# A DLRM tower: tile 0 and the last tile in another order, and matmuls on a constant while TensorE waits for the first rows

## The reference

```python
e = jnp.stack([tbl_0[ids[:, 0]], ..., tbl_26[ids[:, 26]]], axis=1)     # 512 x 27 x 128
interactions = jnp.einsum('bfd,bgd->bfg', e, e)
z = jnp.concatenate([e.reshape(B, -1), interactions[:, _TRIU_I, _TRIU_J]], axis=1)
h = jnp.concatenate([z, dense_ctx], axis=1)                             # 512 x 3823
h = jnp.maximum(h @ W_top1 + b_top1, 0.0)                               # 512 x 512
h = jnp.maximum(h @ W_top2 + b_top2, 0.0)                               # 512 x 256
y = h @ W_top3
```

## Time and profile before

| | us |
|---|---|
| median of 3 runs (lowest, highest) | 192.55 (192.2, 193.46) |
| profiled execution, its own time | 192.25 |
| its span, first to last instruction | 190.5 |
| PE busy | 153.6 (81%) |
| DVE, ACT, POOL busy | 107.6, 106.3, 108.3 |
| mean granted TensorE clock | 0.973 |

### The profile page before, as it was taken

The page is one execution under the profiler, slowest core; times in us unless marked ns, Lnnn a source line. Parts: engine busy times, 40 slices in busy tenths (PEclk is TensorE's granted clock), DMA queues, the critical chain, the costliest instruction groups (busy, mean ns, idle before and its releaser), DMA issues.

```text
span 190.5 us, 2285 instructions
## 1 busy us (share of the span) xinstructions
PE 153.6 (81%) x744; PEld 135.4 (71%) x744; DVE 107.6 (57%) x204; ACT 106.3 (56%) x205; POOL 108.3 (57%) x114
## 2 busy tenths in 40 slices
PE   0033497709998798998999999999999999990885
PEld 0011376608997798897988989988989897970654
DVE  6664777726557975823684852358677203576201
ACT  2673768807459957434789341449836303498111
POOL 4878878787777778777577777766774000000000
PEclk9999999997999999999999999999999999999589
DMA  4988878862335422212122212221221000000000
GB/s 122 293 253 256 220 215 268 238 136 84 91 97 157 115 70 68 55 42 55 41 55 59 54 42 55 57 55 29 59 55 45 0 0 0 0 0 0 3 0 0
DMA packets 10021, 16.40 MB, mean 86 GB/s; under 512 B 3876, under 2 KB 4392, under 8 KB 9956
## 3 DMA queue, kind: packets, MB, share of 16 engines
q1 hardware_dynamic: 6553, 9.17, 15.8%
q0 software_dynamic: 3456, 7.08, 15.2%
HBM read 16.24 MB, written 0.00 MB: 85 GB/s over the span
## 4 chain that ended last, share of the span: by engine, by line
PE 55%; POOL 14%; ACT 10%; issue 8%; DMA 7%; DVE 4%; ACTq 0%
POOL rows L256 14%; PE h_ps L546 10%; PE h_ps L547 9%; PE h_ps L548 9%; ACT stage_a L306 6%; DMA rows<-in_tbl,ids_sb 6%; PE gram_ps L573 5%; PE gram_ps L612 4%; PE h_ps L586 4%; PE h_ps L588 4%; PE h_ps L587 4%; PE tp_ps L531 4%; ACT y L296 3%; DVE y L423 1%; DMA ids_sb<-in_ids 1%
## 5 line engine op out<-in xcount | busy, mean ns | idle before, releaser
L256 POOL DMA_INDIRECT rows<-in_tbl,ids_sb x108 | 107.6, 997 | 36.6 <-issue 30.8
L546 PE MATMUL h_ps<-w_hi,e 128*128 128x512 f32 x108 | 51.2, 475 | 0.0
L412 DVE TENSOR_TENSOR e<-tp_ps,e 128x512 fp32r<-128x512 f32 (+1 forms) x28 | 31.9, 1160 | 26.4 <-ACT e L280 14.4
L547 PE MATMUL h_ps<-w_lo,e 128*128 128x512 f32 x108 | 44.5, 412 | 0.0
L548 PE MATMUL h_ps<-w_hi,e 128*128 128x512 f32 x108 | 44.3, 410 | 0.0
L531 PE MATMUL tp_ps<-ident,rows 128*128 128x128 f32 x108 | 21.7, 304 | 27.1 <-DMA rows<-in_tbl,ids_sb 25.1
L280 ACT ACTIVATE e<-tp_ps 128x512 fp32r<-128x512 f32 (+1 forms) x28 | 28.7, 1056 | 23.0 <-PE tp_ps L531 18.5
L531 PEld LDWEIGHTS tp_ps<-ident,rows 128*128 128x128 f32 x108 | 14.4, 148 | 33.6 <-DMA rows<-in_tbl,ids_sb 19.6
L547 PEld LDWEIGHTS h_ps<-w_lo,e 128*128 128x128 f32 x108 | 33.7, 312 | 0.5
L548 PEld LDWEIGHTS h_ps<-w_hi,e 128*128 128x128 f32 x108 | 33.1, 306 | 0.6
L546 PEld LDWEIGHTS h_ps<-w_hi,e 128*128 128x128 f32 x108 | 33.0, 306 | 0.6
(11 more groups left out here) (43 smaller groups left out, 111.4 us busy)
## 6 DMA issues: line engine op xcount, KB each, us to landing
stage_a<-in_W_top SPq DMA_DIRECT2D x10, 512.0 KB, 4.2
rows<-in_tbl,ids_sb POOLq DMA_INDIRECT x108, 3.4
y<-in_W_top SPq DMA_DIRECT2D x3, 512.0 KB, 4.2
w<-in_W_top SPq DMA_DIRECT2D x1, 512.0 KB, 4.5
w_pairs<-in_W_top SPq DMA_DIRECT2D x11, 28.0 KB
w_pairs<-in_W_top SPq DMA_DIRECT2D x11, 24.0 KB
y<-in_W_top SPq DMA_DIRECT2D x1, 256.0 KB, 4.3
w_pairs<-in_W_top SPq DMA_DIRECT2D x5, 12.0 KB
```

The lines of the kernel that those rows point to most:

```text
L256: nc.gpsimd.indirect_dma_start(rows[:, n % RING, :], None, tables[f], bass.IndirectOffsetOnAxis(ids_sb[:, t, f:f + 1], 0), engine_sem=gath ...
L412: last = nc.vector.tensor_tensor(features(1, fs[0], fs[-1] + 1), tp_ps[k % 2][:, 0:len(fs), :], features(0, fs[0], fs[-1] + 1), ALU.subtract)
L546: nc.tensor.matmul(out, hi, w_hi[:, f, :], start=f == 0, stop=False)
L547: nc.tensor.matmul(out, hi, w_lo[:, f, :], start=False, stop=False)
```

## The change

- Tile 0: PE goes by single features: transpose of f, then the three matmuls of f - 6. Features 21 and 22 come ahead of gram, and four features are left for between its parts.
- Ahead of the first transpose PE does 14 matmuls of 512 columns on a constant, and two after each of the first six transposes; their output is read by no one. DVE sets the constant first (a memset of 640 elements a partition ahead of the one of `w_pairs`).
- The `spacer` memset writes 500 elements a partition, not 250.
- SP issues four pair loads behind each W_top1 load from feature 6 on, 44 of the 73, and the other 29 at the end.
- Last tile: quad 6 is transposed right after feature 12, the gram begins after feature 13 and `layer2(2)`, features 14 to 19 lie between its parts, and features 20 to 26 come after its last part, ahead of `pairs_h1(3)`. ACT and DVE do `split_e(3, 6)` earlier in their order. The outputs of `layer2(2)` and `layer3(2)` lie in other banks, and `copy_y(2)` comes after the second sum of tile 3.

```diff
-        h2T_ps = [gram_ps[:, 512 * m:512 * m + P] for m in range(MC)]
-        y_ps = gram_ps[0:1, 512 * MC:512 * MC + P]
+        def h2T_ps(t, m):
+            bank = m + 2 * (t == NT - 2)
+            return gram_ps[:, 512 * bank:512 * bank + P]
+        def y_ps(t):
+            return h1_ps[t % 2][0:1, 0:P] if t == NT - 2 else gram_ps[0:1, 512 * MC:512 * MC + P]
...
+        PAIRS_PER_W = 4
...
+            pair_loads = list(pair_weight_loads())
             for c in range(0, F, PER_DMA):
...
+                if c == 6:
+                    sp.wait_ge(pairs_zeroed, 1)
+                if c >= 6:
+                    for dst, src in pair_loads[PAIRS_PER_W * (c - 6) // PER_DMA:PAIRS_PER_W * (c - 4) // PER_DMA]:
+                        sp.dma_start(dst, src).then_inc(pairs_loaded, 16)
-            sp.wait_ge(pairs_zeroed, 1)
-            for dst, src in pair_weight_loads():
+            for dst, src in pair_loads[PAIRS_PER_W * (-(-F // PER_DMA) - 3):]:
                 sp.dma_start(dst, src).then_inc(pairs_loaded, 16)
...
                 else:
+                    split_e(t, 6)
                     copy_h1T(u)
                     relu_h2(u)
-                    split_e(t, 6)
...
-                nc.vector.memset(e[:, 0, 0:50, F:ROWS].bitcast(f32), 0.0).then_inc(spaced, 1)
+                nc.vector.memset(e[:, 0, 0:100, F:ROWS].bitcast(f32), 0.0).then_inc(spaced, 1)
...
+            nc.vector.memset(x[:, 0, 0:HC + 1, :].bitcast(f32), 1.0).then_inc(warm_ready, 1)
             nc.vector.memset(w_pairs[:, :, :], 0.0).then_inc(pairs_zeroed, 1)
...
                     copy_h1T(u)
+                    split_e(t, 6)
                     relu_h2(u)
-                    split_e(t, 6)
-                    copy_y(u)
             u = NT - 1
-            sums(u, 0, 5)
+            sums(u, 0, 2)
+            copy_y(u - 1)
+            sums(u, 2, 5)
...
+            def warm_up(n):
+                for _ in range(n):
+                    nc.tensor.matmul(h1_ps[1][:, :], x[:, 0, HC, :], x[:, 0, 0:HC, :].rearrange("p c b -> p (c b)"),
+                                     start=True, stop=True)
+            pe.wait_ge(warm_ready, 1)
+            warm_up(14)
+            for f in range(F):
+                transpose(0, f)
+                if f < 6:
+                    warm_up(2)
+                if f >= 6:
+                    embeddings_h1(0, f - 6, f - 5)
...
+                if u == 0:
+                    embeddings_h1(u, 21, 23)
+                    gram(u, 0)
+                    gram(u, 1)
+                    gram(u, 2)
+                    embeddings_h1(u, 23, 24)
+                    gram(u, 3)
+                    embeddings_h1(u, 24, 25)
+                    gram(u, 4)
+                    transposes(t, 0)
+                    gram(u, 5)
+                    embeddings_h1(u, 25, 26)
+                    gram(u, 6)
+                    embeddings_h1(u, 26, 27)
+                    gram(u, 7)
...
             u = NT - 1
-            grams(u)
+            transposes(u, 6)
+            transpose_h1(u - 1)
+            embeddings_h1(u, 13, 14)
+            layer2(u - 1)
+            gram(u, 0)
+            gram(u, 1)
+            layer3(u - 1)
+            embeddings_h1(u, 14, 15)
+            gram(u, 2)
...
+            embeddings_h1(u, 19, 20)
+            gram(u, 7)
+            embeddings_h1(u, 20, 27)
             pairs_h1(u)
```

More of the change, by code:

```diff
@@ L335, in relu_h2 @@
                 act.wait_ge(h2_done, MC * t + 1)
-                nc.scalar.activation(h2T[:, 0, :], h2T_ps[0], ACT.Relu, bias=b2[:, 0:1]).then_inc(h2_act_ready, 1)
+                nc.scalar.activation(h2T[:, 0, :], h2T_ps(t, 0), ACT.Relu, bias=b2[:, 0:1]).then_inc(h2_act_ready, 1)
             def sums(t, first, end):
@@ L521, in _, with transpose @@
         def _(pe):
-            def transposes(t, q):
+            def transpose(t, f):
+                q, i = divmod(f, QF)
                 k = t * NQ + q
-                if k == 0:
+                n = t * F + f
+                if n == 0:
                     pe.wait_ge(ident_ready, 1)
-                if k >= 2:
+                if k >= 2 and i == 0:
                     pe.wait_ge(e_lo_ready, k - 1)
[L528 to L532, removed]
+                pe.wait_ge(rows_landed[n % RING], 16 * (n // RING + 1))
+                last = nc.tensor.transpose(tp_ps[k % 2][:, i, :], rows[:, n % RING, :], ident[:, :])
+                if f == F - 1:
                     if t == 0:
@@ L535, in transposes, with embeddings_h1 @@
                     last = nc.tensor.transpose(tp_ps[k % 2][0:CTX, QF - 1, :], ctx_sb[:, t, :], ident[:, :])
[L536 to L542, removed]
+                if i == QF - 1 or f == F - 1:
+                    last.then_inc(transposed, 1)
+            def transposes(t, q):
+                for f in quad_features(q):
+                    transpose(t, f)
+            def embeddings_h1(t, first, end):
+                for f in range(first, end):
+                    if f == 0 and t >= 2:
+                        pe.wait_ge(h1_ready, 2 * (t - 1))
+                    if f % QF == 0:
+                        pe.wait_ge(e_lo_ready, t * NQ + f // QF + 1)
                     if t == 0:
@@ L560, in gram @@
                         pe.wait_ge(h1T_act_ready, t)
[L561 to L566, removed]
+                if part == 0 and t >= 2:
+                    pe.wait_ge(h2_act_ready, t - 1)
+                    pe.wait_ge(h2_dve_ready, t - 1)
+                if part == 1 and t >= 2:
+                    pe.wait_ge(y_ready, t - 1)
+                if part == 1 and t == NT - 1:
+                    pe.wait_ge(h2_act_ready, t)
+                    pe.wait_ge(h2_dve_ready, t)
                 if part >= 2:
@@ L611, in layer2 @@
                             pe.wait_ge(y_sum_ready, GP * (t + 2) - 1)
-                        last = nc.tensor.matmul(h2T_ps[m], w2[:, c, m * P:(m + 1) * P], h1T[:, c, :],
+                        if t == NT - 2 and c == 0:
+                            pe.wait_ge(y_ready, t)
+                        last = nc.tensor.matmul(h2T_ps(t, m), w2[:, c, m * P:(m + 1) * P], h1T[:, c, :],
                                                 start=c == 0, stop=c == HC - 1)
@@ L626, in grams @@
                 gram(t, 1)
-                embeddings_h1(t, 5, 0, 1)
+                embeddings_h1(t, 20, 21)
                 gram(t, 2)
-                embeddings_h1(t, 5, 1, 2)
+                embeddings_h1(t, 21, 22)
                 gram(t, 3)
-                embeddings_h1(t, 5, 2, 3)
+                embeddings_h1(t, 22, 23)
                 gram(t, 4)
-                embeddings_h1(t, 5, 3, 4)
-                if t + 1 < NT:
-                    transposes(t + 1, 0)
+                embeddings_h1(t, 23, 24)
+                transposes(t + 1, 0)
                 gram(t, 5)
-                embeddings_h1(t, 6, 0, 1)
+                embeddings_h1(t, 24, 25)
                 gram(t, 6)
-                embeddings_h1(t, 6, 1, 2)
+                embeddings_h1(t, 25, 26)
                 gram(t, 7)
[L641 to L649, removed]
-                grams(u)
+                embeddings_h1(t, 26, 27)
+            def warm_up(n):
[10 more added lines that the diff above has]
+                    embeddings_h1(0, f - 6, f - 5)
+            for u in range(NT - 1):
+                t = u + 1
+                if u == 0:
[13 more added lines that the diff above has]
+                    gram(u, 7)
+                else:
+                    grams(u)
                 transposes(t, 1)
@@ L666, in _ @@
                     pairs_h1(u, 3)
-                embeddings_h1(t, 3)
+                embeddings_h1(t, 12, 13)
                 if t == 1:
+                    embeddings_h1(t, 13, 16)
                     pairs_h1(u)
-                if t < NT - 1:
                     transposes(t, 6)
-                    if t == 1:
-                        embeddings_h1(t, 4)
+                    embeddings_h1(t, 16, 20)
                     transpose_h1(u)
-                    if t > 1:
-                        embeddings_h1(t, 4)
-                else:
+                elif t < NT - 1:
+                    embeddings_h1(t, 13, 16)
+                    transposes(t, 6)
                     transpose_h1(u)
[L679 to L683, removed]
-            u = NT - 1
-            grams(u)
+                    embeddings_h1(t, 16, 20)
+            u = NT - 1
+            transposes(u, 6)
[7 more added lines that the diff above has]
+            gram(u, 2)
+            embeddings_h1(u, 15, 16)
+            gram(u, 3)
+            embeddings_h1(u, 16, 17)
+            gram(u, 4)
+            embeddings_h1(u, 17, 18)
+            gram(u, 5)
+            embeddings_h1(u, 18, 19)
+            gram(u, 6)
+            embeddings_h1(u, 19, 20)
+            gram(u, 7)
+            embeddings_h1(u, 20, 27)
             pairs_h1(u)
```

17 lines of the change are left out of this document (9 added, 8 removed).

## The result

| | us |
|---|---|
| changed kernel, 4 runs | 186.06, 186.71, 191.49, 193.41; median 189.1 |
| a fifth run of it, not in the median | 187.06 |
| kernel before beside it, 4 runs | 192.2 to 193.46, median 192.97 |
| ratio, changed to before | 0.9674, interval [0.9617, 0.9732] |

The ratio leaves the two longest runs of the changed kernel out and takes in 186.06, 186.71 and 187.06; it puts the change at 3.3% faster. Both are needed, since the head differs between them and the tail does not.

The account below looks back on a forecast made before the run. The prediction took PE's holes at both ends, with the clock down behind them, as the bound. From 192.25 us it took 7.3 (tail) and 0.7 (head): 184.25, with the median 0.3 above, 184.5; range 180.6 to 189.5.

Parts of the forecast that it names:

- Tail, 7.3 us forecast: Last tile: gram 5.0 us sooner, x ready at 172.0, PE hole 1 us, pairs at high clock; bounds 5 and 8.
- Rival (d): Last tile: the reorder gives nothing, since ACT's chain, not PE's order, sets x; total 191.9 us; chance 0.06.
- Head, 0.7 us forecast: Start through tile 0: first gram 1.1 us sooner, 1.0 lost to low clock, 0.6 gained at a PE wait.
- I take it as cured: Tile 0 gathers: longer spacer makes eight long ones short, last gather 4.4 us sooner, at 35.0; bounds 0 and 4.4.
- its own signs: Head would be wrong if gathers are long in other places, or rows land after 42 us.
- The pair loads, 45.7 us for the last W_top1 load: DMA queue in the head: 40 pair loads ahead cost 16.4 us, so the last W_top1 load lands at 45.7, not 38.4.
- The 1 us to complete: Last term of the sum for the last W_top1 load's landing: 1 us for the load to complete.
- Rival (a): Head: pair loads hide and rows rule, gram near 43.6 us, POOL 4.4 sooner; total 180.9; chance 0.24.
- first sign: Sign of Rival (a): no wait of ACT for weights; its other sign is PE waiting for rows at 70 us.
- (b): Head: W_top1 loads land later, at 51 to 52 us, gram at 55; 4.8 lost, total 190; chance 0.15.
- (c): Head: each pair load holds the whole queue 0.52 us, last W_top1 load at 59.3, total 198; chance 0.05.
- The constant matmuls, nothing: Start of tile 0: cost 0 to 0.2 us, worth zero, since PE waits for rows anyway.

Follow-up runs that it names:

- the second set of runs: The changed kernel run again with nothing edited, six runs: median 187.19 us (185.72 to 191.72), ratio 0.970 to the kernel before.
- the first profile: Profile of the changed kernel's 193.41 us run, nothing edited, span 191.6 us; the same kernel profiled again ran 185.72 us, span 183.9.

## Why the prediction was right or wrong

**The total** (184.5, range 180.6 to 189.5) came out 1.6 to 2.6 us low by the runs in the ratio (186.06 to 187.06), 2.7 by the median of the second set of runs (187.19), and 4.6 by the median of the first four. The direction and most of the size were right, for the reason given: the last tile.

**Tail, 7.3 us forecast.** Measured 7.0 in the trace and 6.3 by the kernel that has it alone. Its steps held one by one: first gram 4.35 us after the start of feature 12 (4.7 by the sum), x ready 16.6 us after the gram (15.95), a hole of 1.48 (1.0), pair matmuls all at the high level. The 0.7 us between the 16.6 and the 15.95 lie mostly in one gap: gram(3, 2) starts 2.83 us after gram(3, 0) (158.92, 156.09), before 2.00 (163.01, 161.01). The first eight gram matmuls take 1.39 us there instead of 0.99, of which the sum had 0.2, and layer3(2), of which I had written that it adds nothing, stands between gram(3, 1) and feature 14 and takes 0.52 (157.48 to 158.00). The hole was also summed wrong: eight features were put behind the last part of the gram, but feature 19 lies ahead of it, and seven of 0.71 give a hole of 1.7 us, not 1.0. Rival (d) is out.

**Head, 0.7 us forecast, 0.4 lost in one profile, nothing that can be told in the runs.** Here the step that failed is "I take it as cured" of the spacer. I had read the start of the subtraction against the start of the gather (0.05 harmful, 0.34 harmless) and put the new one at 0.26. What goes with it is the start of the memset behind which the subtraction is queued. In the trace before, all eight long gathers have a memset that starts 0.13 or 0.14 us ahead of them; where it starts 0.18 or more after the gather's start, the gather is short. The harmless one of the earlier trace rows:

```profile
25.91 0.27 DVE L396 MEMSET e<- 128x250 f32 x1
```

Over all traces of kernels without the wait, a gather is lengthened where the memset starts between 0.52 us ahead of it and 0.07 after, and not from 0.10 after on; and with the long memset even subtractions at 0.32 after the gather's start hold it up. So a longer memset can only lengthen the hold, to the end of the subtraction plus 0.81: 1.49 became 1.75, 4 us slower by itself. The rows that show it (25.91, 28.09, the gathers beside them) were in my hands. By its own signs the prediction is wrong in the head: gathers are long, the last row is transposed at 47.31, and ACT does not wait for the last W_top1 load. That the first gram comes at 50.22, 0.7 us from the 49.5 forecast, is luck: the rows are late where the weights were expected to be, and in the first profile it comes at 52.78.

Why a gather is held is not shown. The prediction took the long gathers as speaking against the inference that writing descriptors is not hit. But a gather of this kernel also reads its ids from SBUF (`ids_sb`), so that it may be held in that read, and the trace does not tell the two apart.

**The pair loads, 45.7 us for the last W_top1 load.** The direction is right and the size near, but not as the bound of the changed kernel: POOL was so late that SP, which waits for rows, issued the last load at 40.09 and 38.01 in the two profiles, and it landed 5.6 and 7.7 us later. Both give 45.7, the number of the sum, but by a late issue, and ACT did not wait for it. With short gathers the load is the bound, at 46.1 and, with the short spacer, 48.5. The 1 us to complete in the sum is from no row. Rival (a)'s first sign, no wait of ACT for weights, is in the changed kernel, but its early rows are not, and with early rows the weights are late; so (a) is out. So are (b) and (c), whose landings at 51 and 59 us no trace shows. That the pair loads queue on few DMA engines was argued from their mean rate. The cut loads, with the same bytes in ten DMAs more, fit it: big loads went from 10.2 to 5.5 us. The Trainium skill (DMA: Bandwidth & Descriptors, Why a DMA increments its semaphore by 16 and not by 1) says that a load runs on the largest number of engines up to 16 that divides its slowest dimension. By it, as an estimate, the last load was to land at 44.6 us uncut (46.1 and 48.5 measured), and the gain by cutting was to be 5 to 7 us (3 to 4 measured), so it does not give the size; which engines each load ran on is in no view of the profile.

**The constant matmuls, nothing.** Held, as far as the runs can tell. PE stood for 4.41 us ahead of the row at 15.55, and its clock was at the low level again from 14 to 19.5 us (0.50 granted), so they did not carry the high level to the first feature. Without them three features of tile 0 go at the low level, with them one; the rows set the pace either way.

**What was not foreseen is the scatter.** The changed kernel has runs 5 us above its others. The profile of one shows a gather of 4.40 us beside `split_wp` and 2.46 us of PE's wait for it, with the clock low after it: that is the largest item of the 5.1 us that it loses there, and not the whole. That the other long runs have the same cause is not shown, since only that one was profiled. The kernel before lies within 191.84 to 194.78, but for the one run of 188.69, which was not profiled either. The kernels in which DVE waits in `split_wp` still scatter by 2.7 to 3.6 us.

## What to carry to other kernels

If a gather on POOL is longer than its siblings, look at what DVE had queued when the gather began, not only at what it was executing; here a wait of DVE for its own last instruction let POOL in, and a longer filler in front made it worse. Small loads ahead of a big one can hold it up by more than their bytes suggest, so try cutting those whose row counts divide badly before deciding on their order. When several edits share one bound, the worth of one shows only when the others' bound is gone: here DVE's waits were worth nothing while uncut pair loads stood ahead of the weights (187.19 without, 187.52 with), and 6.8 us with the pair loads behind them (190.72 without, 183.88 with).

## What the runs showed of the hardware that was not expected

- A gather (0.94 us) that starts 0.08 us after a memset of DVE (500 elements, 0.47 us), with a subtraction of two SBUF inputs (0.63) queued behind it, takes 1.75 us; 0.13 us after a memset of 250 elements it takes 1.49. Each time it ends 0.81 us after the subtraction. Beside seven such subtractions in a row it took 1.15 and 1.42 in two profiles, and in a third 4.40, 0.81 past the end of all seven. With a semaphore wait between memset and subtraction it takes 0.94, unless the subtraction is already running (up to 1.33 in tile 0 of that kernel). The Trainium skill (SBUF — State Buffer, Who interferes with whom) has a VectorE subtraction of two SBUF inputs meet GpSimd's reads only, and infers that descriptor writing is not hit. The gather both reads ids from SBUF and writes descriptors, so these runs show that an indirect gather is hit, but not by which of the two.
- With short gathers, the big loads (512 KB) took a median of 10.2 us to land with pair loads of up to 26 rows queued among them (10.8 in another trace), and 5.5 with those of over 16 rows cut at 16 (6.2 and 7.1 in two others).
